# The first expert on all tokens of two batches during the first search, in place of its own pass

## The reference

```python
x = x + 0.5 * _L0_ffn_ref(_layernorm(x), gate_w, w_gate, w_up, w_down)
x = x + _L0_attn_ref(_layernorm(x), Wq, bq, Wk, bk, Wv, bv, Wo, bo)
x = x + 0.5 * _L0_ffn_ref(_layernorm(x), gate_w, w_gate, w_up, w_down)
```

```python
gating, idx = jax.lax.top_k(affinity, k)          # k = 256 of 1024, for each batch and expert
x_in = x[bidx, idx]
h = jax.nn.silu(jnp.einsum('bekd,eid->beki', x_in, w_gate)) * jnp.einsum('bekd,eid->beki', x_in, w_up)
x_e = jnp.einsum('beki,edi->bekd', h, w_down)     # inner width 512
out = jnp.zeros_like(x).at[bidx, idx].add(gating[..., None] * x_e)
```

## Time and profile before

| | us |
|---|---|
| median of 3 runs (1190.69 to 1193.63) | 1193.07 |
| profiled execution | 1193.89 |
| its span | 1192.0 |
| PE busy | 1076.0 (90%) |
| DVE busy | 909.0 (76%) |
| ACT busy | 777.0 (65%) |
| POOL busy | 614.0 (52%) |

### The profile page before, as it was taken

How to read it: one execution, slowest core, us unless ns; L and a number is a source line. 1 busy time by engine, 2 the same in 40 slices (tenths; PEclk the granted TensorE clock), 3 DMA queues, 4 the chain that set the end, 5 groups by cost and what they waited for, 6 DMA issues and landing times.

```text
span 1192.0 us, 23693 instructions
## 1 busy us (share of the span) xinstructions
PE 1076.0 (90%) x8860; PEld 466.1 (39%) x8860; DVE 909.0 (76%) x1491; ACT 777.0 (65%) x1471; POOL 614.0 (52%) x626
## 2 busy tenths in 40 slices
PE   6199999998699999999999999999998898899993
PEld 6066676664232222222222222222222255556652
DVE  5746755465889999999999999999997444854441
ACT  3054323432669999999989999899999836222120
POOL 4057888777689401100004446555420187778886
PEclk7589999999799999999999999999999999999997
DMA  9025446458423411122210213112210125445453
GB/s 277 33 64 114 106 100 139 92 128 214 107 86 78 94 44 29 36 62 43 54 33 21 63 42 73 28 27 63 78 45 13 34 75 130 90 96 112 97 102 29
DMA packets 93066, 93.97 MB, mean 79 GB/s; under 512 B 14684, under 2 KB 70108, under 8 KB 92920
## 3 DMA queue, kind: packets, MB, share of 16 engines
q1 hardware_dynamic: 70424, 75.67, 22.5%
q0 software_dynamic: 22528, 16.79, 10.4%
HBM read 64.23 MB, written 30.13 MB: 79 GB/s over the span
## 4 chain that ended last, share of the span: by engine, by line
DVE 45%; PE 30%; issue 9%; POOL 7%; ACT 5%; DMA 2%; another core or an unknown queue 1%; SPq 1%; DVEq 0%; POOLq 0%; ACTq 0%
DVE mx L1921 38%; PE pS L1354 5%; PE pA L1366 5%; POOL out_dram L662 4%; ACT Pt L1177 3%; PE pO L1355 3%; PE pO L1506 3%; PE pS L1355 2%; POOL xg L639 2%; DVE ge L1602 2%; PE pS L1270 2%; PE pA L1334 2%; PE pA L1442 2%; PE pS L1527 2%
## 5 line engine op out<-in xcount | busy, mean ns | idle before, releaser
L1921 DVE TENSOR_REDUCE mx<-pA 128x2 f32<-128x1024 f32 x512 | 585.5, 1217 | 15.9 <-PE pA L1442 11.8
L1177 ACT ACTIVATE Pt<-pS 128x512 f32<-128x512 f32 x1024 | 556.3, 596 | 31.3 <-PE pS L1527 23.1
L1506 PE MATMUL pO<-Pt,Vst 128*16 128x256 f32 x4096 | 322.0, 387 | 12.5 <-ACT U L1168 12.5
L1067 ACT ACTIVATE Pt<-pS 128x512 f32<-128x512 f32 x128 | 76.3, 597 | 195.5 <-PE pS L1354 146.7
L639 POOL DMA_INDIRECT xg<-zd,idx x128 | 127.0, 992 | 142.5 <-DVE idx L1726 71.1
L1442 PE MATMUL pA<-Kst,Qst 48*128 48x512 bf16 x704 | 137.6, 389 | 17.5 <-DVE mx L1921 14.2
L1506 PEld LDWEIGHTS pO<-Pt,Vst 128*16 128x16 f32 x4096 | 68.1, 94 | 204.5 <-issue 108.1
L1527 PE MATMUL pS<-Qst,Kst 51*128 51x512 bf16 x704 | 138.3, 389 | 5.7 <-ACT Pt L1177 2.1
L729 POOL TENSOR_TENSOR mparts<-mx,onesm 128x32 bf16<-128x32 f32 x16 | 4.0, 252 | 267.6 <-DVE mx L1926 211.3
L1354 PE MATMUL pS<-Pt,wg 128*128 128x512 f32 x256 | 136.8, 616 | 4.5 <-DVE Pt L1753 2.5
L1366 PEld LDWEIGHTS pA<-wd,Pt 128*128 128x128 f32 x960 | 113.2, 192 | 15.4 <-issue 15.3
(11 more groups left out here) (234 smaller groups left out, 1233.3 us busy)
## 6 DMA issues: line engine op xcount, KB each, us to landing
wg<-w_gate_dram SPq DMA_DIRECT2D x32, 256.0 KB
wu<-w_up_dram SPq DMA_DIRECT2D x32, 256.0 KB
wd<-w_down_dram SPq DMA_DIRECT2D x32, 256.0 KB
qk<-parts SPq DMA_DIRECT2D x64, 96.0 KB
Kst<-qk SPq DMA_DIRECT2D x132, 32.0 KB
zd<-Z SPq DMA_DIRECT2D x8, 512.0 KB
vp<-pair SPq DMA_DIRECT2D x4, 1024.0 KB, 4.3
Vst<-vp SPq DMA_DIRECT2D x16, 256.0 KB
```

The source lines that it names most:

```text
L1067: S.activation(sg[:, u % 2, :], pG[u % 2], ACT.Silu).then_inc(s_silu, 1)
L1177: S.activation(Pt[:, s % 4, j, r * 512:(r + 1) * 512], pS[:, bank_of(k, 4 * s + 2 * j + r), :], ACT.Exp, scale=SCALE).then_inc(s_exp, 1)
L1506: last = M.matmul(pO[32 * h:32 * h + 16, cols], Vst[k][:, s % 8, h, :], Pt[:, s % 4, h // 2, (h % 2) * 512 + 256 * a:(h % 2) * 512 + 256 * ...
L1921: V.reduce_max(mx2[:, k, 2 * j:2 * j + 2, c, half], pA[ring[q, a] % 2][:, :, :], AX.X).then_inc(s_Ar, 1)
```

## The change

Expert 0 of batches 0 and 1 has no pass of its own any more. Instead all 2048 tokens of the two batches go through its weights while the first search runs, straight from ZT:

- TensorE: 16 steps (`whole_step`, four for each block of 512 tokens) and four times 16 down products (`whole_down`), written out between the rounds of the search. Steps 0 and 1 stand ahead of the transposes of the affinities, step 2 behind the tail's, one step behind each round, and the rest among the ranking and the first two compactions.
- ScalarE: for each step a silu, and a copy of the up product from PSUM into `whole_u`; four copies of the down products into `whole_y`.
- GpSimd: the 16 products (`whole_product`, 128x512 fp32, both inputs in SBUF). `gains(0)` stands behind product 1, `by_slot(0)` behind product 13, the gathers of expert 1 behind product 14 and those of expert 2 behind product 15.
- VectorE: `whole_gains` makes a gain for each token, which is zero where the token isn't among the 256; `whole_sum` adds the gained rows to X in SBUF, 16 instructions of 128x128 at experts 1 (2) and 1 (4).
- SP: stores X of batches 0 and 1 to x1 behind these sums; only the other half of x1 is still copied from x. The first scatter-add, now expert 1's, waits for the stores. Weights of expert 2 are loaded ahead of the stores of Z of batches 2 and 3, those of expert 3 behind the stores of x1.
- The first search has its affinities in `scr`, since ZT is now read by the steps; the experts' loops start at 1, the ten matmuls on ones are gone, and the second pair's logits and transposes are one place later. Its normalisation, at experts 0 and 1 before, is all in expert 1.

The core of the diff:

```diff
-    for n in range(NF):
-        place[divmod(4 + n, 4)] = ("f", 1, n)
-    place[1, 4] = ("g", 1)
+    for n, at in enumerate([(1, 1), (1, 2), (1, 3), (1, 4), (2, 1), (2, 2), (2, 3), (2, 4)] +
+                           [divmod(4 + n, 4) for n in range(8, NF)]):
+        place[at] = ("f", 1, n)
+    place[2, 0] = ("g", 1)
...
+        first_affT = scr[:, 0, :]
+        first_aff = scr[:, 1, :].rearrange("p (c j r) -> p c j r", c=CH, j=8)
+        whole_y = scr[:, 2:4, :].rearrange("p i (k d) -> p (i k) d", d=D)
+        whole_u = Pt[:, 1, 1, :].rearrange("p (i n) -> p i n", i=2)
+        whole_gain = sb("whole_gain", [P, CH, HB], F32)
...
+        whole_hid = [[hid[0][:, i, :] for i in range(IC)], [hid[1][:, i, :] for i in range(IC)],
+                     [U[i // 2][:, i % 2 * 512:(i % 2 + 1) * 512] for i in range(IC)], [hid[0][:, i, :] for i in range(IC)]]
...
+        def step_done(steps, passes, n):
+            return (steps, n + 1) if n < 15 else (passes, 4)
...
-            for h in range(2):
-                sp.dma_start(x1[h], t["x"][h * HB * N:(h + 1) * HB * N, :]).then_inc(s_copy, 16)
+            sp.dma_start(x1[1], t["x"][HB * N:2 * HB * N, :]).then_inc(s_copy, 16)
...
+            load_weights(2)
             store_z(2)
             store_z(3)
+            for b in range(HB):
+                sp.wait_ge(s_sum, b + 1)
+                for i in range(2):
+                    sp.dma_start(x1_in[b][:, 4 * i:4 * i + 4, :], X[:, b * CH + 4 * i:b * CH + 4 * i + 4, :]).then_inc(s_init[b], 16)
...
+                        if j == 1:
+                            pool.wait_ge(s_init[b], 32)
...
+            def whole_product(n):
+                pool.wait_ge(*step_done(s_whole_silu, s_silu, n))
+                pool.wait_ge(s_whole_copied, n + 1)
+                if n >= 12:
+                    pool.wait_ge(s_whole_down, 1)
+                GP.tensor_tensor(whole_hid[n // IC][n % IC], sg[:, n % 2, :], whole_u[:, n % 2, :], ALU.mult
+                                 ).then_inc(*step_signal(s_whole_hid, s_hid, n))
+            for n in range(2):
+                whole_product(n)
             gains(0)
-            gather(0)
+            for n in range(2, 14):
+                whole_product(n)
+            by_slot(0)
+            whole_product(14)
             gather(1)
-            by_slot(0)
+            whole_product(15)
+            gather(2)
             pool.wait_ge(s_aconst, 16 * 10)
             GP.tensor_tensor(bvb[:, :], ones[:, :], bvc[:, 0:1].to_broadcast([P, D]), ALU.mult).then_inc(s_bvb, 1)
-            for it in range(RUN):
+            for it in range(1, RUN):
                 if it + 2 < RUN:
                     gather(it + 2)
-                if it:
+                if it > 1:
...
+            def whole_silu(n):
+                act.wait_ge(*step_done(s_whole_gate, s_gate, n))
+                if n >= 2:
+                    act.wait_ge(*step_done(s_whole_hid, s_hid, n - 2))
+                S.activation(sg[:, n % 2, :], pG[n % 2], ACT.Silu).then_inc(*step_signal(s_whole_silu, s_silu, n))
+                act.wait_ge(*step_done(s_whole_up, s_up, n))
+                S.activation(whole_u[:, n % 2, :], pU[n % 2], ACT.Copy).then_inc(s_whole_copied, 1)
+            def whole_rows(t):
+                act.wait_ge(*block_done(s_whole_down, s_down, t))
+                S.activation(whole_y[:, 4 * t:4 * t + 4, :].rearrange("p k d -> p (k d)"), pY, ACT.Copy
+                             ).then_inc(*block_signal(s_whole_y, s_ye, t))
+            for n in range(2, 5):
                 front(0, n)
-            act.wait_ge(s_lexp, 1)
-            S.activation(warm[:, :], sd[:, 0:8], ACT.Silu)
-            turn_tokens(0)
-            for it in range(RUN):
+            for n in range(2):
+                whole_silu(n)
+            for n in range(5, 7):
+                front(0, n)
+            for n in range(2, 13):
+                whole_silu(n)
+            whole_rows(0)
+            whole_silu(13)
+            whole_rows(1)
+            for n in range(14, 16):
+                whole_silu(n)
+            whole_rows(2)
+            deviation(2)
+            deviation(3)
+            whole_rows(3)
+            act.nop().then_inc(s_xt, 1)
+            turn_tokens(1)
+            for it in range(1, RUN):
...
-                if (it, k) == (0, 1):
-                    deviation(2)
-                    deviation(3)
-                if (it, k) == (0, 3):
+                if (it, k) == (1, 0):
                     normalise(2, 0, 4)
-                if (it, k) == (0, 4):
+                if (it, k) == (1, 1):
                     normalise(2, 4)
-                if (it, k) == (1, 0):
+                if (it, k) == (1, 2):
                     normalise(3, 0, 4)
-                if (it, k) == (1, 1):
+                if (it, k) == (1, 3):
                     normalise(3, 4)
...
+            def whole_step(n):
+                t, i = divmod(n, IC)
+                if n == 0:
+                    pe.wait_ge(*was_read(("f", 0, 3)))
+                    pe.wait_ge(s_w[0], 32)
+                if n >= 2:
+                    pe.wait_ge(*step_done(s_whole_hid, s_hid, n - 2))
+                M.matmul(pG[n % 2], wg[0][:, i * P:(i + 1) * P], ZT[:, t * 512:(t + 1) * 512], start=True, stop=True
+                         ).then_inc(*step_signal(s_whole_gate, s_gate, n))
+                M.matmul(pU[n % 2], wu[0][:, i * P:(i + 1) * P], ZT[:, t * 512:(t + 1) * 512], start=True, stop=True
+                         ).then_inc(*step_signal(s_whole_up, s_up, n))
+            def whole_down(t, first, end):
+                if first == 0:
+                    pe.wait_ge(*step_done(s_whole_hid, s_hid, 4 * t + 3))
+                    if t == 0:
+                        pe.wait_ge(s_wd[0], 16)
+                        pe.wait_ge(*was_read(("f", 0, 4)))
+                    else:
+                        pe.wait_ge(*block_done(s_whole_y, s_ye, t - 1))
+                for m in range(first, end):
+                    k, i = divmod(m, IC)
+                    last = M.matmul(pY[:, k * D:(k + 1) * D], whole_hid[t][i][:, k * P:(k + 1) * P], wd[0][:, i, :],
+                                    start=(i == 0), stop=(i == IC - 1))
+                if end == 16:
+                    last.then_inc(*block_signal(s_whole_down, s_down, t))
+            for n in range(2, 5):
                 front(0, n)
+            for n in range(2):
+                whole_step(n)
+            for n in range(5, 8):
+                front(0, n)
+            whole_step(2)
             pe.wait_ge(s_const, 16 * 8)
-            for n in range(8, NF):
-                front(0, n)
-            compact(0)
+            for r in range(ROUNDS):
+                front(0, 8 + r)
+                whole_step(3 + r)
+                if r >= 2:
+                    whole_down(0, 2 * (r - 2), 2 * (r - 1))
+            whole_step(13)
+            front(0, 8 + ROUNDS)
+            whole_down(1, 0, 6)
+            front(0, 9 + ROUNDS)
+            whole_down(1, 6, 11)
+            front(0, 10 + ROUNDS)
+            whole_down(1, 11, 16)
+            whole_step(14)
+            pe.nop().then_inc(s_comp, 1)
             compact(1)
-            warm_up(10)
-            turn_tokens(0)
-            for it in range(RUN):
+            whole_step(15)
+            compact(2)
+            whole_down(2, 0, 16)
+            whole_down(3, 0, 16)
+            pe.nop().then_inc(s_xtr, 1)
+            turn_tokens(1)
+            for it in range(1, RUN):
...
-                if (it, k) == (0, 2):
-                    scale_and_shift(2)
-                    scale_and_shift(3)
+                if (it, k) == (1, 2):
+                    whole_sum(0)
+                if (it, k) == (1, 4):
+                    whole_sum(1)
...
+            def whole_gains():
+                V.scalar_tensor_tensor(whole_gain[:, :, :], slotT[:, :, 0].rearrange("p (c b) -> p c b", b=HB), 0.0,
+                                       half[:, :, :].rearrange("p c (b e) -> p c b e", b=HB)[:, :, :, 0],
+                                       ALU.is_ge, ALU.mult).then_inc(s_whole_gain, 1)
+            def whole_sum(b):
+                dve.wait_ge(s_whole_gain, 1)
+                dve.wait_ge(*block_done(s_whole_y, s_ye, 2 * b + 1))
+                for c in range(CH):
+                    last = V.scalar_tensor_tensor(X[:, b * CH + c, :], whole_y[:, b * CH + c, :], whole_gain[:, c, b:b + 1],
+                                                  X[:, b * CH + c, :], ALU.mult, ALU.add)
+                last.then_inc(s_sum, 1)
+            for n in range(5):
                 front(0, n)
-            first_experts(0)
+            for n in range(7, NF):
+                front(0, n)
+            dve.nop().then_inc(s_onehot, 2)
+            dve.nop().then_inc(s_row, 1)
+            dve.nop().then_inc(s_idx, 1)
+            all_onehots(1)
+            pick(1)
+            all_onehots(2)
+            pick(2)
             moments(2)
```

(6 more changed lines are left out.)

71 lines of the change are left out of this document (40 added, 31 removed).

## The result

Nine runs of each kernel on the same chip: 1198.62 us (median) after, 1195.28 before; ratio 1.0032, 95% interval 1.0017 to 1.0046. The change makes the kernel slower by some 3.8 us, 0.3%. One of the nine runs of the changed kernel (1275.3, mean clock 0.833) is left out of the ratio. The profiled execution took 1196.76, span 1195.0. Timed again later, the same pair gave 1.0055 (1.0037 to 1.0072).

A forecast was written before the change was run, and what follows sets the result against it. Expert 3's start, set by the search's VectorE-matmul chain and first experts, was taken to shift the end: clean -2.5, held rounds +7.5, ranking +2.5, so +7.5 on 1193.89; less 0.8 to the median, 1200.6 us, range 1189 to 1210.

The forecast's parts named there:

- Start of the search, +1.2: Before the first round: steps 0 and 1 delay the copies of affinities, part of it hidden; +1.2 us.
- some 3.6 us: Time after a dense TensorE start until the granted clock came back, read behind expert 0's start at 67.62.
- Rounds cost TensorE nothing: In the search: TensorE's 2.28 us of work fits under the round's 2.36, so 0 added.
- The +0.5 for the gains: In the search: the gains stand between products 1 and 2 on GpSimd; once +0.5 us, bounds 0 and 1.
- The clock at 1 from 25 us on: In the search: a granted clock near 1 from 25 us on, named as a sign of the forecast.
- The hold, +7.5: In nine round intervals: GpSimd products hold cand (+1.15) and thr (+0.96) in alternate rounds; +7.5 us, bounds 0 and +11.4.
- Tenth round to compaction, +2.6, +0.3 and +2.5: Ranking: TensorE steps and down products ahead of its matmul +2.6, last down products +0.3, GpSimd holding VectorE +2.5 us.
- Compaction to expert 1, 14.1 (61.3 to 75.4): First compaction to expert 1's first product: index 1.4 us, then gathers, product 15, down products and copies 12.7.
- Experts 1 and 2, 28.5 again: Expert 1's start to expert 3's: down products saved but ScalarE's work waited for; unchanged 28.5 us, bounds -3.6 and +2.
- Sum at expert 3, +7.5: Shift of expert 3's start: clean -2.5, holds in rounds +7.5 and in ranking +2.5, together +7.5 us.
- that the products miss the small instructions: Rival in the search: GpSimd products miss VectorE's small instructions, so rounds aren't held; 1192 us, chance 0.20.
- That the clock stays at 1.2 GHz in the search: Rival in the search: TensorE stays slow, a round holding 4.3 us of its work; 1209 us, chance 0.08.

The follow-up runs named there:

- the matmuls alone: Kernel before plus two unused 128x512 matmuls on TensorE behind each of the ten rounds' matmuls: 1200.15 us, ratio 1.0049.
- the order: Changed kernel with step 15, the last down blocks, product 15, ScalarE's copy and the moments reordered behind the ranking: 1203.67 us, ratio 1.0076 to the kernel before.
- the ranking alone: Changed kernel with the ranking's first matmul ahead of step 13 and by_slot (experts 3 to 7) behind gather 1: 1205.20 us, ratio 1.0077 to the kernel before.
- the quarter's length: Changed kernel with its 16 GpSimd products over only 128 of 512 columns: 1197.50 us, ratio 1.0022 to the kernel before.
- products alone: Kernel before plus one unused 128x512 GpSimd product in each of rounds 2 to 10: 1204.33 us, ratio 1.0089.
- Moves that each looked right: Changed kernel with products 2 to 10 waiting for cand, plus reordering in and behind the ranking; all together 1191.46 us, ratio 0.9975 to the kernel before.
- two fillers of 0.9 us: Changed kernel with products 2 to 10 waiting for cand, plus unused 128x512 matmuls ahead of and behind compaction 1: 1193.65 us, ratio 0.9992 to the kernel before.
- the changed kernel again: The changed kernel without any edit, timed and traced once more: 1200.41 us, ratio 1.0055 to the kernel before.

## Why the prediction was right, and where its terms were off

The prediction was right in its sign and in the mechanism that it gave most chance, and its time (1200.6 against 1198.62) is near. That the time is so near is in part luck. The forecast was +7.5; the two ratios give +3.8 and +6.6, the stages +5.3. The kernel before, timed beside the changed one, had a median of 1195.28 instead of the 1193.07 that the forecast built on, and the two largest misses (the search 3.2 too high, the way to expert 1 2.2 too low) have opposite signs. By its steps:

- **Start of the search, +1.2**: +0.8 over two traces of each. Right. Traces of one program differ by 0.4 to 1.0 here (29.10 and 29.47; 28.12 and 28.93; 30.43 and 29.40); the later ones of the changed kernels had the lower clock between 22 and 26 us. The reading behind "some 3.6 us" is loose: in the first trace of before the clock still read 1.00 up to 68.0, fell there, and was back at about 71.4.
- **Rounds cost TensorE nothing**: right, shown by the matmuls alone (2.36). The +0.5 for the gains didn't come on top: the first interval is 2.91 like the others. The clock at 1 from 25 us on: right.
- **The hold, +7.5, is the mis-sized term**: the nine rounds cost +4.8. It was to be 1.15 at `cand` and 0.96 at `thr` in alternate rounds. Measured: `cand` took 0.67 and 0.71 in turn, 0.51 and 0.55 above its own 0.16, and `thr` wasn't held (but 0.25 once, at 31.27). Part of the miss is that a held instruction ends with the product, so its own 0.16 must not be added: 1.15 was 0.99 at most. The step that failed is "that round's own product starts at its f + 2.71, before the shifted `thr`". With a hold h, `thr` starts at f + 1.87 + h, so this needs h > 0.84, and the prediction took the first product to meet a round that nothing had held. Here the gains held the first round (0.29 at `cand`, 0.25 at `thr` by product 2). Below 0.84 another rule holds, which I didn't look for: the next round starts at f + 2.36 + h, its `cand` at f + 2.83 + h, and the product ends at f + 4.03 (worked out: 3.98), so the next hold is 4.03 - 2.83 - 0.16 - h = 1.04 - h. Two holds in a row add up to 1.04, whatever the first was; nothing settles. The traces bear it out: 0.51 and 0.55 in turn in the changed kernel, 0.53 each time in the runs with the order and the ranking alone (rounds of 2.89), and with the quarter's length, whose product ends at f + 3.22, 0.24 and 0.01 in turn where the rule gives 0.23 for the two. What the search would have done with an unheld first round no run shows. The Trainium skill (SBUF — State Buffer, section "SBUF: two separate sides") has the lock as exclusive; every held `cand` ended with the GpSimd instruction within 0.03 us. It agrees, here and with products alone.
- **Tenth round to compaction, +2.6, +0.3 and +2.5**: +5.1 in all. The ranking's first matmul came 3.99 behind the tenth round instead of 1.36: +2.6 as worked out. The rest is +2.4 (8.39 instead of 5.95), where 2.8 were expected.
- **Compaction to expert 1, 14.1 (61.3 to 75.4)**: 17.6 and 15.7. The index took 2.7 instead of 1.4, since product 14 held the one-hots of the second half (two in 2.37 us, 1.29 unheld). From the index to expert 1 it is 13.0 in the second trace (12.7 worked out; its terms add up to 12.9) and 14.9 in the first, with down block 2 at 1.2 GHz. I had priced no drop of the clock there.
- **Experts 1 and 2, 28.5 again**: 28.3. Right.
- **Sum at expert 3, +7.5**: +5.3. The rounds were 3.2 too high (8.0 with the gains, against 4.8), the way from the compaction to expert 1 2.2 too low (-7.2 against -5.0), and the rest 1.1 too high in three small terms.
- **"A shift of that moment goes through to the end"**: right to within the drift of the clock. The shift was constant from expert 6 to 905 us in the first trace (6.2 to 6.5), with 3.0 left at the end of the span, most of what came back being the drop of the clock near 1000 us in the first trace of before; a second trace kept 6.2 at the last expert, and two traces of before drift by 1 to 3 us. A prediction of 3 us can't be read from one trace's end.
- **Rivals**: that the products miss the small instructions is out. That the clock stays at 1.2 GHz in the search is out; it fell behind the search instead.

What is open: how much of the time difference is the clock. The five stages give +5.3 at expert 3; the two ratios give +3.8 and +6.6 (1.0055 of 1194.3).

## What to carry to other kernels

An idle engine isn't free to use: before work is put on GpSimd beside a serial chain of small VectorE instructions, lay its start and end over one round of that chain, look which instructions with two SBUF inputs it meets, and follow the phase over several rounds, from the round that is held first, instead of adding up single meetings. A semaphore that starts the product with the one long instruction that isn't held gave back 3.75 of 4.8 us in the rounds. Moves that each looked right gave nothing on their own: the ranking's gain was lost behind the next item in GpSimd's order, and the order alone was 3.3 us slower than the changed kernel on the same chip, behind a pause that is unexplained. Together they brought expert 3 from 112 or 113 us to 104.

## What the runs showed of the hardware that I had not expected

- A CAST of 128x4 from SBUF (`idx`), with one input, is held too: 0.92 instead of 0.17, from 64.98 to 65.90, beside a GpSimd product that ran from 64.60 to 65.86. The scan over 1024 columns beside a whole product was not (1.28), nor were reads of PSUM.
- TensorE idled 1.12 and 0.96 us ahead of the two halves of the compaction, and the granted clock then went from 1.00 to 0.50 in four traces of five, for 3 to 10 us; in the one trace with two fillers of 0.9 us it stayed. In the changed kernel's own two traces the same gaps gave 0.66 once and 1.00 once (70 to 80 us).
- A pause of TensorE of 3 us that no semaphore ends (82.34), with the signal of its last matmul late by as much. A shorter delay of that signal, 0.9 and 1.2 us before ScalarE's copy, stands behind down block 2 in two other traces (the changed kernel again and the ranking alone), none in five. The cause is open.
